# Projecting the keys and values of all heads in the layernorm's program, and loading them in the attention units

## The reference

```
qkv = xn @ W_qkv                       # q: 2048 columns, k: 1024, v: 1024
q, k, v by heads; k and v repeated for two query heads
scores = q @ k.T / 8 + slope * (key position - query position), causal softmax
s = (softmax @ v).reshape(B, S, 2048) @ W_out
```

## Time and profile before

| | |
|---|---|
| median of 3 runs | 3356.93 us (3354.94 to 3363.76) |
| the profiled execution | 3356.11 us, span 3354.3 us |
| busy, share of the span | PE 93%, PE weight loads 71%, DVE 67%, ACT 61%, POOL 35% |
| layernorm | 0 to 45 us |
| first attention | 45 to 1476 us |
| expert networks | 1476 to 2027 us |
| start of the recurrence | 2027 us |

### The profile page before, as it was taken

The page is one execution under the profiler, slowest core; times in us unless marked ns, Lnnn a source line. Parts: engine busy times, 40 slices in busy tenths (PEclk is TensorE's granted clock), DMA queues, the critical chain, the costliest instruction groups (busy, mean ns, idle before and its releaser), DMA issues. The chain is left out here.

```text
span 3354.3 us, 75760 instructions
## 1 busy us (share of the span) xinstructions
PE 3130.9 (93%) x23170; PEld 2393.5 (71%) x23170; DVE 2236.8 (67%) x6696; ACT 2052.0 (61%) x4941; POOL 1164.7 (35%) x1836
## 2 busy tenths in 40 slices
PE   4999999999999999989999996969999974999995
PEld 3676777767767677768888884536666664999995
DVE  5888888888888888876656664547766726333334
ACT  4777777777777777765565553316666643333333
POOL 4444444444444444443333330034232202333331
PEclk9999999999999999999999998979999976999998
DMA  3111111111111111134333332111111133223225
GB/s 89 34 36 33 26 35 36 36 33 36 36 33 36 36 35 34 36 112 139 125 128 116 132 125 70 44 50 29 35 40 42 42 99 115 39 37 88 39 37 170
DMA packets 143913, 208.80 MB, mean 62 GB/s; under 512 B 29762, under 2 KB 101826, under 8 KB 143778
## 3 DMA queue, kind: packets, MB, share of 16 engines
q1 hardware_dynamic: 130914, 189.46, 18.8%
q0 software_dynamic: 12864, 17.57, 3.2%
HBM read 123.22 MB, written 39.98 MB: 49 GB/s over the span
## 5 line engine op out<-in xcount | busy, mean ns | idle before, releaser
L770 POOL TENSOR_SCALAR at_p<-at_p,at_recip 128x512 f32<-128x512 f32 (+3 forms) x1030 | 536.6, 539 | 824.6 <-DVE at_recip L917 824.6
L826 ACT ACTIVATE at_p<-at_p,at_nmax 128x512 f32<-128x512 f32 (+3 forms) x1032 | 570.5, 555 | 130.4 <-DVE at_nmax L911 124.0
L911 DVE CUSTOM_DVE_ANT_0 at_p<-at_s_ps,at_bias 128x512 f32<-128x512 f32 (+3 forms) x1032 | 462.1, 488 | 63.2 <-PE at_s_ps L1043 44.5
L1043 PE MATMUL at_s_ps<-at_k_twice,at_q 64*128 64x512 f32 (+3 forms) x3096 | 341.8, 340 | 3.1 <-DVE at_nmax L911 3.1
L1902 DVE CUSTOM_DVE_ANT_0 aa_a_ps<-aa_a_ps,aa_hidden 128x128 f32<-128x128 f32 (+3 forms) x512 | 242.3, 512 | 118.4 <-PE aa_a_ps L2066 116.2
L1065 PE MATMUL at_o_ps<-at_pT,at_v 128*64 128x512 f32 (+3 forms) x2064 | 306.5, 439 | 0.0
L923 DVE COPY at_pT<-at_t_ps 128x512 f32<-128x512 f32 (+3 forms) x512 | 239.0, 488 | 94.1 <-PE at_t_ps L1055 90.2
L1802 ACT ACTIVATE aa_pT<-aa_b_ps 128x512 f32<-128x512 f32 (+1 forms) x384 | 197.4, 529 | 145.3 <-PE aa_b_ps L2084 139.1
L1055 PEld LDWEIGHTS at_t_ps<-ident,at_p 64*128 64x128 f32 x5120 | 189.2, 138 | 120.3 <-issue 120.3
L449 ACT ACTIVATE nw_h<-nw_h_ps,nw_b 128x512 f32<-128x512 f32 x192 | 132.2, 689 | 210.9 <-PE nw_h_ps L553 210.4
L526 DVE SCALAR_TENSOR_TENSOR nw_hl<-nw_h,nw_coef_now,nw_hh 128x512 fp32r<-128x512 f32 x192 | 150.1, 782 | 163.9 <-ACT nw_hh L454 163.9
(11 more groups left out here) (307 smaller groups left out, 7772.4 us busy)
## 6 DMA issues: line engine op xcount, KB each, us to landing
at_k_twice<-at_k_twice SPq DMA_DIRECT2D x130, 256.0 KB, 2.8
nw_w_raw<-in_w_all_dram SPq DMA_DIRECT2D x26, 1024.0 KB, 5.1
nw_w_raw<-in_w_all_dram SPq DMA_DIRECT2D x52, 512.0 KB, 6.9
w_all<-in_w_dram SPq DMA_DIRECT2D x12, 768.0 KB, 10.1
nw_xh<-xh_dram SPq DMA_DIRECT2D x10, 512.0 KB, 4.3
nw_xl<-xl_dram SPq DMA_DIRECT2D x10, 512.0 KB, 5.0
at_w_raw<-in_w_heads_dram SPq DMA_DIRECT2D x18, 256.0 KB, 3.8
nw_x<-in_x_dram SPq DMA_DIRECT2D x9, 512.0 KB, 6.0
```

What stands on the lines that cost most here:

```text
L770: pool.tensor_scalar(p, p, recip[:, u:u + 1], 1.0, ALU.mult, ALU.mult).then_inc(scaled, 1)
L826: act.activation(p_sb[:, u, 0:N], p_sb[:, u, 0:N], ACT.Exp, bias=nmax[:, u:u + 1], scale=-1.0, accum_out=total[:, u:u + 1]).then_inc(exped, 1)
L911: dve.tensor_tensor_reduce(out=p_sb[:, u, 0:N], in0=s_ps[u % 2][:, score_at(u // 2)], in1=bias[:, u % 2, S - N:S], scale=1.0, scalar=BIG, ...
L1043: ins = pe.matmul(s_ps[h][:, score_at(j)], qst[par][rows, q, at], k_twice[par][rows, k, 0:N], start=(i == 0), stop=(i == 2))
```

## The change

Keys and values of all 16 heads are projected for a batch as soon as its xh and xl are there, inside the layernorm's program. For each batch there are 8 key jobs (two heads each, 128 columns of weights against 512 rows of x) and 8 value jobs (128 rows of x against 512 columns of weights, so that the values come out with the rows on the partitions and `turn_v` is not needed), six matmuls each. Five PSUM banks go round (`BANKS`). Keys go through three SBUF buffers (`KST`): ACT writes the high part, DVE the remainder, and SP stores the two heads with two transfers of 64 partitions, 256 KB each. Values go through two buffers, each stored with one transfer of 128 partitions, 1 MB in pieces of 1 KB. All of it goes to k_dram (33.55 MB) and v_dram (16.78 MB). In the last batch the values come first and the gate's choice (`choose`) moves to DVE's start of it.

In the attention `project_kv`, `turn_v`, `take_k`, `take_v`, `k_rest`, `values` and `copy_k` are gone. SP loads the keys of unit t+2 twice (once for each half of the partitions) when all scores of unit t are made, and the values of unit t+1 when weigh(t-1) is done. `add_out` moves to the place after the first two masks and works on unit t-2. The banks m_ps have fixed roles (0 queries, 1 and 2 outputs). The first head's query weights are split in the layernorm's program (by POOL, at the third batch). The clearing of pT (L877 before) moves behind the first `q_rest`.

Both changed prologues also load the Sqrt table early on ACT. The recurrence's loads x first, takes the root first, makes the decay factors afterwards (the logarithm without DVE's two steps), and waits for the two weight matrices on PE alone.

```diff
+KST = 3
+BANKS = 5
...
+def projection_order():
+
+    order = []
+    for n in range(B):
+        keys = [("k", n, g) for g in range(KV_GROUPS)]
+        values = [("v", n, i) for i in range(TT * KV // SIDE)]
+        order.extend(keys + values if n < B - 1 else values + keys)
+    return order
+
...
+            def store_keys(n, g):
+                c = key_no(n, g)
+                sp.wait_ge(k_low, c + 1)
+                for e in range(2):
+                    sp.dma_start(k_dram[(2 * g + e) * B + n], keys[c % KST][HD * e:HD * e + HD].bitcast(F32))\
+                        .then_inc(k_stored[c % KST], 16)
+
+            def store_values(n, side):
+                sp.wait_ge(v_out, value_no(n, TT * side) + TT)
+                heads = SIDE // HD
+                sp.dma_start(v_view[n][:, heads * side:heads * side + heads, :],
+                             values[side][:].rearrange("p j i d -> p j (i d)")).then_inc(v_stored[side], 16)
+
...
+            load_x(0)
+            sp.dma_start(wk_raw[:], w_k).then_inc(wk_loaded, 16)
+            load_x(1)
+            sp.dma_start(wv_raw[:], w_v).then_inc(wv_loaded, 16)
+            load_x(2)
+            sp.dma_start(wg[:], w_gate.rearrange("(k p) e -> p k e", p=P)).then_inc(loaded, 16)
+            sp.dma_start(bg[:], b_gate.rearrange("(a e) -> a e", a=1).broadcast_to([B, E0])).then_inc(loaded, 16)
+            sp.dma_start(al[:], alpha.broadcast_to([B, 1])).then_inc(loaded, 16)
+            sp.dma_start(wq_raw[:], w_q[0]).then_inc(wq_loaded, 16)
...
+            def split_values(side):
+                at = slice(SIDE * side, SIDE * side + SIDE)
+                pool.tensor_scalar(wvh[:, :, at], wv_raw[:, :, at], 1.0, 1.0, ALU.mult, ALU.mult).then_inc(wv_high, 1)
+                pool.wait_ge(wv_high, side + 1)
+                pool.tensor_tensor(wvl[:, :, at], wv_raw[:, :, at], wvh[:, :, at].bitcast(F32), ALU.subtract)\
+                    .then_inc(wv_split, 1)
+
...
+            def key_low(n, g):
+                c = key_no(n, g)
+                dve.wait_ge(k_high, c + 1)
+                dve.tensor_tensor(keys[c % KST][:, 1, :], bank_of(("k", n, g))[:], keys[c % KST][:, 0, :].bitcast(F32),
+                                  ALU.subtract).then_inc(k_low, 1)
...
+            def key_high(n, g):
+                c = key_no(n, g)
+                act.wait_ge(projected, PLACE["k", n, g] + 1)
+                if c >= KST:
+                    act.wait_ge(k_stored[c % KST], 32 * (c // KST))
+                act.activation(keys[c % KST][:, 0, :], bank_of(("k", n, g))[:], ACT.Copy).then_inc(k_high, 1)
+
+            def take_values(n, i):
+                side, tile = divmod(i, TT)
+                act.wait_ge(projected, PLACE["v", n, i] + 1)
+                if tile == 0 and n > 0:
+                    act.wait_ge(v_stored[side], 16 * n)
+                act.activation(values[side][:, :, tile, :], bank_of(("v", n, i))[:].rearrange("p (j d) -> p j d", d=HD),
+                               ACT.Copy).then_inc(v_out, 1)
...
+            def bank_free(job):
+
+                if PLACE[job] >= BANKS:
+                    kind, n, i = ORDER[PLACE[job] - BANKS]
+                    pe.wait_ge(k_low if kind == "k" else v_out, (key_no if kind == "k" else value_no)(n, i) + 1)
+
+            def project_keys(n, g):
+                job = ("k", n, g)
+                if n == 0:
+                    pe.wait_ge(wk_split, g // 2 + 1)
+                bank_free(job)
+                cols = slice(P * g, P * g + P)
+                for a, (w, x) in enumerate([(wkh, xh), (wkl, xh), (wkh, xl)]):
+                    if a == 2:
+                        pe.wait_ge(low, n + 1)
+                    for k in range(KT):
+                        ins = pe.matmul(bank_of(job)[:], w[:, k, cols], x[:, k, n * S:n * S + S],
+                                        start=(a == 0 and k == 0), stop=(a == 2 and k == KT - 1))
+                ins.then_inc(projected, 1)
+
...
+            for n in range(B):
+                more = n + 1 < B
+                pe.wait_ge(high, KT * n + KT)
+                if not more:
+                    pe.wait_ge(loaded, 48)
+                    for k in range(KT):
+                        ins = pe.matmul(l_ps[0:B, 0:E0], xsum[:, k, :], wg[:, k, :], start=(k == 0), stop=(k == KT - 1))
+                    ins.then_inc(ready, 1)
+                    for i in range(2 * TT):
+                        project_values(n, i)
+                for g in range(KV_GROUPS):
+                    if g == 6 and more:
+                        turn(n + 1)
+                    project_keys(n, g)
+                if more:
+                    for i in range(2 * TT):
+                        project_values(n, i)
...
+            def load_keys(unit, par):
+                for e in range(2):
+                    sp.dma_start(k_twice[par][HD * e:HD * e + HD, :, :].bitcast(F32),
+                                 k_dram[ds(unit, 1)].rearrange("a p h q -> (a p) h q")).then_inc(k_loaded[par], 16)
+
+            def load_values(unit, par):
+                sp.dma_start(v[par][:].rearrange("p i d -> p (i d)"), v_dram[ds(unit, 1)].rearrange("a p c -> (a p) c"))\
+                    .then_inc(v_loaded[par], 16)
...
-                            copy_k(kv_count(j * B + pair * 2 + (par + 2)), par)
+                            t = j * B + pair * 2 + par
+                            sp.wait_ge(scored, t * 8 + 8)
+                            load_keys((t + 2) % UNITS, par)
+                            sp.wait_ge(summed, t + 1)
+                            load_values((t + 1) % UNITS, 1 - par)
...
+            take_q(1, 0)
+            take_q(2, 1, bank=1)
...
-                    take_k(kv_count(t + 2), par)
                     turn_out(t, 0, par)
-                    take_v(v_count(t + 1), par)
                     exps(t + 1, 0)
...
+            dve.memset(m_ps[2][:], 0.0)
+            dve.memset(v[1][:], 0.0).then_inc(v_loaded[1], 16)
...
-                k_rest(t + 2, par)
-                dve.wait_ge(summed, t + 1)
-                values(v_count(t + 1), 1 - par)
+                add_out(t + (-2), b_before, 1)
+                add_out(t + (-2), b_before, 0)
...
-                add_out(t + (-1), par, b_before, 1)
-                add_out(t + (-1), par, b_before, 0)
...
+            dve.wait_ge(proj_out, 2)
+            dve.memset(m_ps[1][:], 0.0)
+            dve.memset(pT[1][:], 0.0).then_inc(zeroed, 1)
...
-                turn_v(t + 1, 1 - par)
...
-                project_out(par, lambda: pe.wait_ge(o_low, t + 1), lambda: pe.wait_ge(vT_out, t + 3),
-                            lambda: pe.wait_ge(proj_out, q_count(t + 2)))
-                if new_keys is not None:
-
-                    pe.wait_ge(w_split, new_keys * 2 + 1)
-                project_kv(t + 3, par, b_keys, next_unit)
-
-            pe.wait_ge(zeroed, 1)
-            pe.wait_ge(w_split, 2)
-            project(m_ps[0], P, 0)
-            project(m_ps[1], 0, 0)
-            values_free(0)
-            turn_v(0, 0)
+                project_out(par, lambda: pe.wait_ge(o_low, t + 1), lambda m: pe.wait_ge(proj_out, out_left(t + (-2), m)),
+                            next_unit)
+
+            pe.wait_ge(w_split, 1)
+            project(m_ps[0], 0, 0)
+            project(m_ps[1], 0, 1)
             pe.wait_ge(proj_out, 2)
...
-            sp.dma_start(gam[:], row(decay)).then_inc(w_loaded, 16)
-            sp.dma_start(la[:], row(log_alpha)).then_inc(w_loaded, 16)
-            for i in range(2):
-                sp.dma_start(x_in[i][:], x_view[i]).then_inc(x_loaded[i], 16)
+            sp.dma_start(x_in[0][:], x_view[0]).then_inc(x_loaded[0], 16)
+            sp.dma_start(gam[:], row(decay)).then_inc(gam_loaded, 16)
+            sp.dma_start(la[:], row(log_alpha)).then_inc(gam_loaded, 16)
+            sp.dma_start(x_in[1][:], x_view[1]).then_inc(x_loaded[1], 16)
...
-            act.wait_ge(w_loaded, 64)
+            act.wait_ge(cleared, 1)
+            act.activation(early[:], eps[:, 0:1], ACT.Sqrt)
+            roots(0)
+            act.wait_ge(gam_loaded, 32)
             act.activation(gam[:], gam[:], ACT.Exp, scale=-1.0).then_inc(act_chain, 1)
-            act.wait_ge(dve_chain, 2)
-            act.activation(gam[:], gam[:], ACT.Ln).then_inc(act_chain, 1)
-            act.wait_ge(dve_chain, 3)
-            for h in range(RH):
-                act.activation(factor[:, h, :], ahead[:], ACT.Exp, scale=gam[:, h:h + 1], bias=la[:, h:h + 1])\
-                    .then_inc(act_chain, 1)
-            act.wait_ge(cleared, 1)
-            roots(0)
+            act.wait_ge(act_chain, 1)
+            act.activation(gam[:], gam[:], ACT.Ln, bias=1.0).then_inc(act_chain, 1)
             take_turn(0, 0)
             take_turn(0, 1)
+            act.wait_ge(act_chain, 2)
+            act.wait_ge(dve_chain, 1)
+            for h in range(RH):
+                act.activation(factor[:, h, :], behind[:], ACT.Exp, scale=gam[:, h:h + 1], bias=la[:, h:h + 1])\
```

(67 more changed lines are left out.)

372 lines of the change are left out of this document (191 added, 181 removed).

## The result

The changed kernel takes 3296.49 us (median of four runs, 3293.89 to 3297.14), the kernel before 3356.48 on the same chip (four runs, 3354.94 to 3363.76). The ratio is 0.9821, 95% interval 0.981 to 0.9833: 60 us faster, where the point of the forecast was 44.

| stretch | before | after | change | forecast |
|---|---|---|---|---|
| layernorm's program, its end | 45.2 | 213.8 | +168.6 | +182.6 |
| attention, start to first units' output | 35.4 | 26.8 | -8.6 | -10 |
| 128 units, first to last output | 1391.85 | 1180.48 | -211.4 | -208.6 |
| recurrence's program | 182.5 | 173.9 | -8.6 | -8 |
| network's program | 551.3 | 552.4 | +1.1 | 0 |

A forecast was written before the change was run, and what follows sets the result against it. PE, never idle in the 128 units, was taken as the bound, and key stores in the layernorm's program afterwards. Sum: 182.6 - 208.6 - 10 - 8 = -44.0 us, 3356.9 to 3313 us; range 3287 to 3338 (0.8).

The forecast's parts named there:

- rival A: Layernorm's program: key stores as fast as 128-partition ones, PE the bound, end at 211, total 3296 us; chance 0.24.
- The signs listed for the forecast: Layernorm's program: DMA share near 1 at some 240 GB/s, PE below 95%, ACT's key copy waiting for a store.
- The units: The attention's 128 units: without project_kv and turn_v each saves 1.63 us, period 9.25 us, 208.6 us less.
- The slack: In each unit, between DVE's last mask and PE's next score(0): falls from 1.9 us to 0.5 us.
- Rival B: The units shrink less: a wait of 0.15 to 0.3 us each before score(0), 26 us, total 3339; chance 0.16.
- The layernorm's program: Stores bound it: 207.5 us of DMA time, end at 228 us, attention starts 182.6 us later (166 to 205).
- the rate of the key stores: Layernorm's program: 64-partition key stores run at 221 GB/s, copy_k's rate for a full DMA share, taking 151.8 us.
- A second size: Layernorm's program: PE alone done at 205 us, with turnings 8.4 us and early half clock 2.6 us.
- Rival C: Layernorm's program: the three key buffers wait for queued landings, cycle 9.6 us, 53 us more, total 3366; chance 0.06.
- Rival D: Layernorm's program: PE falls to half clock waiting for banks, at worst 146 us more, some 3440; chance 0.03.
- The prologues: Attention's: first mask at 11.9 us after its start, 10 us less; recurrence's: dots start at about 17 us, 8 less.

The follow-up runs named there:

- the last kernel: The changed kernel with one 128-partition store per key group, four key buffers, pT cleared by POOL and slopes loaded first: 3288.22 us, ratio 0.9792.

## Why the prediction was right, and where its sum was off

**Sign, place and size.** 60 us faster against 44, inside the range. But 3296 lies in the band that was given to rival A (3288 to 3303, chance 0.24) and not in the forecast's own (3303 to 3324, chance 0.48): the range held because it was drawn to take in A. The signs listed for the forecast were mostly absent: DMA share near 1 at some 240 GB/s with PE below 95% was expected, and 0.88, 282 GB/s and PE at 99% came; only ACT's waits for stores were there. (The forecast's own terms, 52.95 MB in 207.5 us, would also make 255 GB/s and not 240.) Of the 16 us between, 14.9 stand in the trace: 14 in the layernorm's program, 2.8 in the units and 0.6 in the recurrence, less the 1.4 that the attention's prologue gave too little and 1.1 in the network. The medians add the rest.

**The units** (-208.6, measured -211.4). Both savings were read from the spacing of matmuls and not from their record lengths, and the 0.10 us for a change of shape stayed, as left in. The slack was forecast to a hundredth (0.48 and 0.49), and the run with DVE's extra instruction showed that it is that link. Rival B did not come: by that run (0.6 us more gave 0.11) its 0.2 us a unit would have needed some 0.7 us more on DVE.

**The layernorm's program** (+182.6, measured +168.6). The step that failed is the rate of the key stores, "keys 33.55 MB / 221 = 151.8 us". The 221 came from a stretch in which copy_k used a single half, and for one half it holds (209 measured). But key stores alternate between the halves, and the two together reach 274 GB/s: 33.55 MB / 274 = 122 us, 29 less than in the sum. With that the stores' floor is no longer 17 us above PE's (228 against 211) but near it: the sum with 122 us gives 199, the run with PE's work cut gave 206. What the 7 us between are made of no run separates; the DMA share of 0.90 in that run speaks for holes in the queue, which the sum did not count. A second size was off the other way round: PE alone is done at 200.1 and not 205. In the run with one store its 186.8 us from 13.27 on are 178.7 for the 128 jobs (1.396 each), 1.6 for the early clock (forecast 2.6), 0.87 for each of seven turnings and 0.4 for the gate, where I had 1.2 a turning and 1 for the rest.

The Trainium skill (SBUF — State Buffer, "Can I just issue two DMAs to hit both halves?") says that two transfers, one for each half, gained 6%. For the pair the measurement decides: 274 against 209 is 31%, in stretches with keys alone. Its limit for one half, some 218 GB/s (section Door 1: The DMA port swizzle), agrees with the 209 measured here. Its way out, one transfer over all partitions, agrees: 371 GB/s with three buffers, 406 with four.

**Rival A** had the right number, 3296, by two mistakes that cancel. It took the stores to be as fast as those of 128 partitions, in which case the end would have been 205.8 and not its 211. The real end of 213.8 is PE's, plus 3.2 us of bank waits and a tail 4.8 longer. The 2.8 us by which that is later than A's 211 were given back by the units, which gained 2.8 more than the sum had.

**Rival C** asked for a cycle of 9.2 us in the ring; it is 3 x 1.9 = 5.7. **Rival D**: PE stayed at full clock in the changed kernel's middle (1.00). Over the middle of the program the clock sank clearly, to 0.89 and 0.91, only where a third of PE's work was taken away with the pair of stores kept.

**The prologues** (-10 and -8, both -8.6). In the attention's, DVE's row came out as listed up to the biases, done 6.1 us after the start (forecast 6). What I left out is PE's clock between first mask and units. The next twelve score matmuls take nearly twice as long as at the same place before: the granted clock over them is 0.50, the lower level (1.2 GHz), against 1.00, the upper one (2.4 GHz). First before, then changed:

```profile
68.46 0.95 PE L1043 MATMUL at_s_ps<-at_k_twice,at_q 64*128 64x128 f32 x12 [1.56 <-DVE at_nmax L911]
```
```profile
227.36 1.65 PE L1211 MATMUL at_s_ps<-at_k_twice,at_q 64*128 64x128 f32 x12 [4.89 <-DVE at_nmax L1099]
```

PE's wait of 4.89 us while DVE clears pT looks like the reason, but it does not decide it. With the clearing on POOL PE waits as briefly as before, and the matmuls take 1.65 us all the same:

```profile
224.43 1.65 PE L1211 MATMUL at_s_ps<-at_k_twice,at_q 64*128 64x128 f32 x12 [1.56 <-DVE at_nmax L1100]
```

One thing that differs from before in both is that PE did less ahead of them: before, it had 18 more projection matmuls there (its rows from 59.9 to 65.9 us), for keys and values, which the change has taken out of the prologue. No run isolates that, so the reason stays open. The first mask is followed by the units after 9.2 us and not the 8.0 of the earlier trace rows. With the 0.4 us by which the first mask came late, less 0.1 up to the first output, that is the 1.4 us. In the recurrence's prologue the root came 0.9 us sooner than forecast and the dot products 0.2.

## What to carry to other kernels

When two chains of work move into one stretch, work out the floor of each; where they come out close, as 206 and 206 here, the end can lie above both (8 us in this one case, of which 4.8 are a tail that also depends on what the last batch makes last), and speeding up one alone gives little: 60 us less of PE's work gave 7.7, faster stores 8.0, both together 37. A DMA rate read from one row belongs to that row's pattern: ask which partitions the transfers ahead of and behind it touch. And a layout in memory that lets a tile leave in one transfer over all partitions cost under 1 us here besides a changed index (8.0 us sooner in the program, 7.2 over the whole).

## What was not expected of the hardware

- Stores from 64 partitions: 209 GB/s if all come from one half, 274 if they alternate between the halves, whether from one queue or from two (289 and 291 GB/s over the middle of the program); from 128 partitions at once 371 with three buffers and 406 with four, while a fourth buffer leaves the pair at 268.
- Two bias instructions of DVE took 3.13 us beside POOL's clearing of 128x4096, ending 0.7 us after it, and 0.89 without it; in the last kernel it was 3.16 us.
- PE's twelve score matmuls after the first mask ran at the lower clock (1.65 us against 0.95) whether PE had waited 4.89 us ahead of them or 1.56.
- The network's program took 17 us longer in one kernel that differs only in who issues key stores 1200 us earlier. This stays open.
